# Order of the set-up before the first normalization of a two-layer conv/FFN kernel

## What is computed

```
x = x + L0_conv(_ln_c(x), w_d, w_u, w_r, w_l)
t = _to_tokens(x)
t = t + L0_ffn(_ln_t(t), gate_w, gate_b, weight1, weight2)
x = _from_tokens(t, x)
x = x + L1_conv(_ln_c(x), w_d, w_u, w_r, w_l)
t = _to_tokens(x)
t = t + L1_ffn(_ln_t(t), W, V, gamma, beta)
x = _from_tokens(t, x)
```

## Time and profile before

| | |
|---|---|
| median of 3 runs | 4314.11 us (4312.28 to 4323.86) |
| the profiled execution, span | 4315.0 us |
| PE busy / ACT busy / DVE busy | 97% / 47% / 31% of the span |
| chain that ended last | 93% on PE |
| first matmul on x | 20.16 us |
| first ACTIVATE of ACT | 22.49 us |
| first matmul of the sweeps | 144.54 us |

### The profile page before, as it was taken

One profiled execution on the slowest core, in us unless ns is written; L12 is line 12 of the kernel. 1 busy time (PEld: TensorE's weight loads), 2 busy tenths in 40 slices (PEclk: granted clock), 3 DMA queues, 4 the chain that ended last, 5 costly groups with the idle time before them and its releaser, 6 DMA issues.

```text
span 4315.0 us, 139757 instructions
## 1 busy us (share of the span) xinstructions
PE 4170.7 (97%) x57266; PEld 3076.9 (71%) x57266; DVE 1330.3 (31%) x2528; ACT 2016.0 (47%) x8972; POOL 119.6 (3%) x243
## 2 busy tenths in 40 slices
PE   7999999999989999999999899999999999999999
PEld 2799999995342699999995266666666666666665
DVE  3555533334555655533334700000000000000000
ACT  5002334334554102243344366666666666666666
POOL 1000000000000000000000000000000000000000
PEclk8899999999999999999999899999999999999999
DMA  5000000002447200000005400000000000000000
GB/s 138 17 0 0 0 0 0 0 0 74 133 113 216 61 0 0 0 0 0 0 0 143 124 15 21 15 21 21 15 21 21 15 21 21 15 21 21 15 21 18
DMA packets 178401, 144.32 MB, mean 33 GB/s; under 512 B 110910, under 2 KB 177502, under 8 KB 178014
## 3 DMA queue, kind: packets, MB, share of 16 engines
q1 hardware_dynamic: 178014, 138.21, 12.1%
HBM read 79.19 MB, written 58.98 MB: 32 GB/s over the span
## 4 chain that ended last, share of the span: by engine, by line
PE 93%; DVE 3%; issue 2%; ACT 2%; SPq 1%; DMA 0%; ACTq 0%; DVEq 0%; PEldq 0%
PE ps L930 22%; PE ps L767 21%; PE ps L745 18%; PE ps L835 16%; PE ps L830 3%; PE ps L571 3%; PE ps L563 1%; PE ps L582 1%; PE ps L592 1%; PE ps L718 1%; PE ps L606 1%; DVE rstd L1162 1%; PE ps L808 1%; PE ps L636 1%; PE ps L685 1%
## 5 line engine op out<-in xcount | busy, mean ns | idle before, releaser
L930 PEld LDWEIGHTS ps<-xl,vt 65*32 65x32 f32 x28800 | 1036.0, 108 | 717.0 <-ACT xl L1145 686.2
L1145 ACT ACTIVATE xl<-ps 64x8 f32<-64x8 f32 x7200 | 1176.5, 170 | 656.8 <-PE ps L930 652.8
L930 PE MATMUL ps<-xl,vt 65*32 65x8 f32 x28800 | 1422.6, 183 | 20.6
L835 PE MATMUL ps<-idle 128*32 128x256 bf16 (+1 forms) x5894 | 1374.9, 273 | 0.0
L767 PE MATMUL ps<-xl,taps 128*128 128x128 f32 (+2 forms) x7880 | 921.3, 280 | 4.7 <-DVE xl L1334 4.7
L767 PEld LDWEIGHTS ps<-xl,taps 128*128 128x128 f32 x7880 | 920.8, 191 | 5.6 <-issue 5.3
L745 PE MATMUL ps<-split 128*128 128x400 f32 x4140 | 781.0, 352 | 12.8 <-DVE split L1329 12.8
L745 PEld LDWEIGHTS ps<-split 128*128 128x128 f32 x4140 | 779.0, 190 | 16.5 <-issue 15.2
L1418 DVE TENSOR_TENSOR xl<-xl 64x320 f32<-64x320 f32 x180 | 125.1, 695 | 1709.1 <-PEq L934 1699.7
L1003 ACT ACTIVATE img<-xl 128x144 f32 x788 | 365.8, 464 | 556.5 <-DVE xl L1311 556.5
L835 PEld LDWEIGHTS ps<-idle 128*32 128x32 bf16 x5894 | 584.5, 99 | 22.1 <-issue 10.2
(11 more groups left out here) (153 smaller groups left out, 1685.0 us busy)
## 6 DMA issues: line engine op xcount, KB each, us to landing
ring<-in_x_dram SPq DMA_DIRECT2D x144, 200.0 KB, 3.7
x_dram<-sums SPq DMA_DIRECT2D x144, 200.0 KB, 3.2
t_dram<-sums SPq DMA_DIRECT2D x72, 200.0 KB, 3.6
ring<-t_dram SPq DMA_DIRECT2D x72, 200.0 KB, 3.9
ring<-x_dram SPq DMA_DIRECT2D x72, 200.0 KB, 3.7
xl<-x_dram SPq DMA_DIRECT2D x45, 320.0 KB, 4.6
out_dram<-xl SPq DMA_DIRECT2D x45, 320.0 KB, 3.5
img<-in_L_ffn_weight_dram SPq DMA_DIRECT2D x4, 512.0 KB
```

The costliest lines, as they stand in the source:

```text
L835: pe.matmul(PS[bank][0:32, 0:n], idle[:, 0:32], idle[:, 0:n], start=True, stop=True)
L930: last = pe.matmul(PS[2 * s + h][c * 32:(c + 1) * 32, t * HB:(t + 1) * HB], vt[:, c * 32:(c + 1) * 32], prev, start=False, stop=True, skip ...
L1145: act.activation(yb[0:64, s % 2, h * HB:(h + 1) * HB, t], PS[s % 2 * 2 + h][0:64, t * HB:(t + 1) * HB], ACT.Sigmoid).then_inc(step_y[h][s ...
```

## The change

- SP issues the x loads of the first norm first. The small loads that nothing needs early (gate_b, gamma, beta) come behind all x loads of that norm (`late_constants`, with a semaphore `late_dma`, for which ACT waits ahead of the second norm and DVE ahead of the batch norm).
- ACT issues gate_w, W and V and the four convolution weights from its own queue, then waits for `consts`, and runs one square root of one element (`warm`) ahead of the norm. It no longer waits for `taps_ready[0]` there.
- POOL fills `idle`, `ident`, `average` and `eps` and sets `consts`; then `pick` and `tables_ready`; then `gate`, `taps`, `fold`, `ones`, `pooled` and the diagonals of `fold`, and `tables_ready` again; then `spread32` as before.
- PE runs 12 idle matmuls behind `consts`, then waits for `centre_ready` and `tables_ready`, and enters the norm. The weight work is in `prepare_weights`, in five parts behind the units 2 to 6: the gate; W and V; nine taps; nine taps; the small product. The idle matmul behind the variances of the first norm runs only from unit 8 on.
- `row_squares` lies behind the weights in `xl`, and the tap transposes of layer 0 use banks 5, 6 and 7.

```diff
-        row_squares = [xl[:, j * CH:(j + 1) * CH] for j in range(SQUARES)]
+        row_squares = [xl[:, 4 * C * KT + j * CH:4 * C * KT + (j + 1) * CH] for j in range(SQUARES)]
...
+        def late_constants(sp):
             for q in range(4):
+                sp.dma_start(gbias[q * E:(q + 1) * E, :], gate_b.rearrange("(e a) -> e a", a=1)).then_inc(late_dma, 16)
+            for h in range(2):
+                sp.dma_start(half(gb, h)[:, 0:1], gamma.rearrange("(e a) -> e a", a=1)).then_inc(late_dma, 16)
+                sp.dma_start(half(gb, h)[:, 1:2], beta.rearrange("(e a) -> e a", a=1)).then_inc(late_dma, 16)
...
         @block.sync
         def _(sp):
-            sp.dma_start(graw[:, :], gate_w).then_inc(setup_dma, 16)
...
-            sp_norm(sp, 0)
+            sp_norm(sp, 0, meanwhile=lambda: late_constants(sp))
...
-            for buf, value in ((ident, 0.0), (average, 0.0), (fold, 0.0), (gate, 0.0), (taps, 0.0), (ones, 1.0),
-                               (pooled, 1.0), (idle, 0.0)):
-                alone(pool.memset(buf[:, :], value))
+            for buf in (idle, ident, average):
+                alone(pool.memset(buf[:, :], 0.0))
...
+            pool.affine_select(out=ident[:, :], in_=ident[:, :], compare_op=ALU.not_equal, fill=1.0, base=0,
+                               pattern=[[-1, 128]], channel_multiplier=1).then_inc(consts, 1)
+            alone(pool.memset(pick[:, :], 0.0))
+            for h in range(2):
+                alone(pool.memset(half(pick, h)[:, 126 + h:127 + h], 1.0 / C))
+            pool.sem_inc(tables_ready, 1)
+            for buf, value in ((gate, 0.0), (taps, 0.0), (fold, 0.0), (ones, 1.0), (pooled, 1.0)):
+                alone(pool.memset(buf[:, :], value))
...
-            if i == 0:
+            if i == 0 and n >= 8:
                 keep_clock(pe, 512, SPARE)
...
+        def prepare_weights(pe, part):
+            if part == 0:
+                pe.wait_ge(setup_dma, 16)
+                pe.transpose(PS[7][0:C, 0:E], graw[:, :], ident[0:E, 0:E]).then_inc(gate_t, 1)
+            elif part == 1:
+                pe.wait_ge(rdma, 32)
+                pe.wait_ge(gate_ready, 1)
+                for a in range(2):
+                    last = pe.transpose(PS[7][0:64, 64 + a * 64:128 + a * 64], wraw_r[:, a * 64:(a + 1) * 64], ident[0:64, 0:64])
+                last.then_inc(rnn_t, 1)
+            elif part < 4:
+                pe.wait_ge(rnn_w_ready, 1)
+                pe_taps(pe, 0, part - 2)
+            else:
+                pe.wait_ge(wcp[0], 6)
...
+                if i == 0 and 2 <= n <= 6:
+                    prepare_weights(pe, n - 2)
...
             pe.wait_ge(consts, 1)
-            pe.wait_ge(setup_dma, 80)
...
+            for _ in range(12):
+                keep_clock(pe, 512, SPARE)
             pe.wait_ge(centre_ready, 1)
...
+            pe.wait_ge(tables_ready, 1)
             pe_row_norm(pe, 0)
...
         @block.scalar
         def _(act):
-            act.wait_ge(setup_dma, 80)
+            act.dma_start(graw[:, :], gate_w).then_inc(setup_dma, 16)
+            act.dma_start(wraw_r[:, 0:64], rnn_w).then_inc(rdma, 16)
+            act.dma_start(wraw_r[:, 64:128], rnn_v).then_inc(rdma, 16)
+            load_taps(act, 0)
             act.wait_ge(consts, 1)
-            act.wait_ge(taps_ready[0], 1)
+            act.activation(warm[:, :], eps[0:1, 0:1], ACT.Sqrt)
             act_row_norm(act, 0)
...
+            act.wait_ge(late_dma, 128)
             act_token_norm(act, 1)
...
             dve.wait_ge(gate_t, 1)
+            dve.wait_ge(tables_ready, 2)
...
+            dve.wait_ge(late_dma, 128)
             link(dve.tensor_tensor(bnm[:, 6:7], bnm[:, 5:6], gb[:, 0:1], ALU.mult), 3)
```

More of the change, by code:

```diff
@@ L153, in b2_at @@
             return slots[0:1, 1, b, a:a + n * C]
+        late_dma = sem("late_dma")
         setup_dma, consts, gate_t, gate_ready = sem("setup_dma"), sem("consts"), sem("gate_t"), sem("gate_ready")
-        centre_ready, pick_ready, spread_ready = sem("centre_ready"), sem("pick_ready"), sem("spread_ready")
+        centre_ready, tables_ready, spread_ready = sem("centre_ready"), sem("tables_ready"), sem("spread_ready")
         wdma, wtr, wcp, taps_ready = ([sem(f"{n}{l}") for l in range(2)] for n in ("wdma", "wtr", "wcp", "taps_ready"))
@@ L199, in metaformer @@
         bn_std, rnn_c = sem("bn_std"), sem("rnn_c")
[L200 removed]
+        pool_done = sem("pool_done")
         passed = sem("passed")
@@ L498, in _ @@
                 alone(pool.memset(half(pick, h)[:, 126 + h:127 + h], 1.0 / C))
+            pool.sem_inc(tables_ready, 1)
+            for buf, value in ((gate, 0.0), (taps, 0.0), (fold, 0.0), (ones, 1.0), (pooled, 1.0)):
+                alone(pool.memset(buf[:, :], value))
+            for base in (0, 64, -64):
+                alone(pool.affine_select(out=fold[:, :], in_=fold[:, :], compare_op=ALU.not_equal, fill=0.5, base=base,
+                                         pattern=[[-1, 128]], channel_multiplier=1))
+            pool.sem_inc(tables_ready, 1)
             ones_at = sums[:, 0:5 * 128]
             alone(pool.memset(ones_at, 0.0))
-            pool.sem_inc(pick_ready, 1)
             for q in range(4):
@@ L514, in _ @@
             pool.wait_ge(ln[1].var, 2 * UNITS)
-            pool.memset(taps[:, :], 0.0).then_inc(taps_blank, 1)
-            pool.wait_ge(taps_blank, 1)
+            alone(pool.memset(taps[:, :], 0.0))
             place_taps(pool, 1)
@@ L535, in _, with tap_at, pe_taps @@
             stage_segment(pool, 0, 0, 0)
-        TAP_BANKS = (((4, 5, 6), (4, 5, 6)), ((2, 3, 4), (5, 6, 7)))
-        def pe_taps(pe, l):
+        TAP_BANKS = (((5, 6, 7), (5, 6, 7)), ((2, 3, 4), (5, 6, 7)))
+        NINTH = (256, 0)
+        def tap_at(l, a, k):
+            c = k % 4 * 128 + (NINTH[l] if k == KT - 1 else 0)
+            return PS[TAP_BANKS[l][a][k // 4]][0:64, c:c + 128]
+        def pe_taps(pe, l, a):
             pe.wait_ge(wdma[l], 64)
             wk = wraw[l].rearrange("p (a i k) -> p a k i", a=2, k=KT)
[L542 to L548, removed]
+            for k in range(KT):
+                if l == 0 and a == 1 and k % 4 == 0:
+                    pe.wait_ge(wcp[l], k // 4 + 1)
+                last = pe.transpose(tap_at(l, a, k), wk[:, a, k, :], ident[:, :])
+                if k % 4 == 3 or k == KT - 1:
+                    last.then_inc(wtr[l], 1)
         def variances(pe, i, n, squares):
@@ L672, in pe_token_norm @@
                     centre_and_project(n, 1)
+        def prepare_weights(pe, part):
[14 more added lines that the diff above has]
+                for h in range(2):
+                    last = pe.matmul(PS[7][h * 64:(h + 1) * 64, 192:256], half(centre, h)[:, h * 64:(h + 1) * 64],
+                                     half(wbd, h)[:, h * 64:(h + 1) * 64], start=True, stop=True)
+                last.then_inc(rnn_c, 1)
         def pe_row_norm(pe, i):
@@ L821, in pooling @@
             if g == NG - 1:
-                pe_taps(pe, 1)
+                for a in range(2):
+                    pe_taps(pe, 1, a)
             pe.wait_ge(pool_read, g + 1)
```

39 lines of the change are left out of this document (8 added, 31 removed).

## The result

The changed kernel takes 4289.22 us (median of 4 runs, 4286.89 to 4296.33), the kernel before 4316.10 us (median of 4, 4312.28 to 4323.86). The ratio is 0.9939, with a 95% interval of 0.9927 to 0.9951: 26.9 us, 0.62%, faster. The profiled execution of after took 4290.47 us, its span 4288.7 us. The two spans are 26.3 us apart.

The account below looks back on a forecast made before the run. Serial set-up, then x loads, then PE were taken as bounds; earlier means (13.8 us) and two table loads (1.3 us each), less 4.0 us in first units, gave 12.4 us gained: 4301.7 us, range 4294.5 to 4309.0 us.

Parts of the forecast that it names:

- What bounds the kernel now: First 145 us: serial set-up, x loads pace units 0 to 10, PE bounds from unit 12; root difference carries to the end.
- POOL, ACT and the weights' places: Set-up: `consts` at 3.57 us, ACT's issues end about 5 us, second table load goes; weights between units cost 3.5 us.
- The rival of dear issues: Norm start: x waits in shared engines or ACT's issues are dear; about 3 us less gained, 4304.7 us, chance 0.12.
- PE's entry: PE's start: 12 idle matmuls at 0.227 us take 2.7 us, so PE is free at 6.3 us.
- The rival of a start at 1.2 GHz: PE's start: idle matmuls take 5.4 instead of 2.7 us, first means at 9.0 us; 4303.8 us, chance 0.05.
- The transposes: Weight work between first-norm units: nine transposes cost PE 1.93 us, and late means delay later x loads.
- The trip of a load: First norm, units 0 to 10: means n + 3 start about 4.7 us after means n end.
- The clock: Behind the first root: PE's fall to 1.2 GHz is kept; a 10.2 us stretch costs some 3.5 us.
- Nothing changed behind it: Everything behind the sweeps' first matmul, itself forecast 12.4 us sooner near 132.1 us, stays unchanged.
- The slower rival: First units: clock falls and stays low until the idle matmuls ahead of the last group; 4351 us, chance 0.04.
- The rival of a drain: ACT's table switch costs a drain besides the load; 1.3 us more gained, 4300.4 us, chance 0.03.
- The rival of hidden transposes: First norm: transposes hide in PE's waits for loads; root at 27.2 us, 4298.2 us, chance 0.10.

Follow-up runs that it names:

- weights_behind_x: The changed kernel with the seven weight loads issued by SP behind the first six x loads, not by ACT: 4290.81 us, ratio 0.9932.
- no_idle: The changed kernel without the 12 idle matmuls at the start, 24 spare semaphore increments in their place: 4291.58 us, ratio 0.9934.
- before_again: The kernel before, unchanged, run once more: 4316.01 us, ratio 0.9995.
- no_warm_root: The changed kernel without the one-element square root ahead of the norm: 4293.80 us, ratio 0.9942.
- before_code_as_after: The kernel before with 8 idle matmuls instead of 16 and spare increments: one on PE, one on DVE, six on ACT; 4306.59 us, ratio 0.9983.
- weights_ahead: The changed kernel with all five parts of the weight work ahead of the first unit, behind the 12 idle matmuls: 4296.09 us, ratio 0.9957.

## Why the prediction was wrong, and where it was right

**What bounds the kernel now** stood. The set-up is serial, and the 13.4 us won at the first root were still there at the sweeps.

**POOL, ACT and the weights' places.** `consts` at 3.57 us as forecast. ACT's seven issues take 0.41 to 0.67 us each and end at 5.08 us (about 5 forecast), one table load at 5.11 us, none behind it. The rival of dear issues falls. The small late loads and `place_taps` (ends at 25.3 us, 27 forecast) lie outside the path to the reciprocal at 30.40 us.

**PE's entry was wrong.** Forecast 2.7 us for 12 idle matmuls and the first means at 6.35 us; measured 4.34 us and 7.84 us. PE starts at 1.2 GHz. In weights_behind_x the twelve take 5.30 us, 0.44 us each, and in no_idle the first means run at half rate. Here my reading of the trace failed: I took a granted clock of 1.00 at 12 us and a mean of 0.227 us as the engine's state at its first matmul. The column shows 1.00 up to the first recorded change, also where the durations show the lower level. In before the first record is a rise at 16.24 us, behind 4 us of transposes at the low rate and just ahead of the idle matmuls at 16.60 us, which so took 3.63 us. In before_again the rise is recorded at 20.16 us, and they took 5.30 us. In after it is recorded at 6.79 us, in the middle of the twelve. The Trainium skill, "TensorE: Matmul & The Clock Gate", section "What's actually happening", has the throttled state as the default. These durations agree with it, and the prediction's sentence that the trace speaks against it was wrong. The rival of a start at 1.2 GHz, given 0.05, is what happened at this point: it had the first means at 9.0 us, which weights_behind_x nearly reaches with 8.81 us.

**The transposes were wrong the other way.** Nine were to take 1.93 us each time; they take 1.20 us, because the earlier trace rows gave the low rate and after runs them at the high one. Unit 2 was to have its means at 9.9 us and had them at 11.67 us, 2.20 us of it waiting for its load, beyond even the late bound of 11 us. The errors cancel:

| means of unit | forecast | measured |
|---|---|---|
| 0 | 6.35 | 7.84 |
| 2 | 9.9 | 11.67 |
| 5 | 17.3 | 17.75 |
| 7 | 22.4 | 21.43 |
| 10 | 28.05 | 27.23 |
| first root | 30.7 | 29.75 |

The late start and the late x together make unit 2 1.8 us late; each nine transposes give 0.7 us back. The trip of a load held: unit 10 starts 4.9 us behind the end of the means of unit 7 (22.36 us), where 4.7 us were forecast. From the first means to the root the sum had 24.35 us, and it took 21.91 us. The root is 13.4 us sooner (12.4 forecast). That this term is so near was luck: it is made from two errors that cancel. Against the mean of the old starts the step, read at the reciprocal, is 15.4 us. The starting point of the sum, the root at 43.14 us, was taken from one execution, the quickest of six.

**The clock.** A fall was kept behind the root: it came, at 34.1 us, for 6.8 us, and was 10.2 us long before. The low stretches that began before the sweeps sum to 37.6 us instead of 47.8 us. From the root to the sweeps another 3.2 us were gained. The difference in the clock is large enough for them, but no run separates the two. That the difference at the root is carried unchanged to the end was wrong there. By the same sum all six profiles with the old start have 44 to 51 us of low clock, the eight with the changed start 27 to 44 us. Which part of the change moves the falls is not settled: no edit here moved them alone, and two kernels whose root came 1.9 and 8.1 us later than after's had the least of it.

**"Nothing changed behind it" is the step that failed by the most.** Two column sweeps are 3.5 and 3.6 us shorter, because the code in front of them has another length. The prediction put this at nothing, and no rival held it. The account is: 13.4 to 15.4 us at the root and some 7 us from code places. The 4 to 6 us that are left of the 26.9 us I put down to the clock's low stretches and to the chance of single executions; this rest was not measured by itself.

The slower rival, PE kept at 1.2 GHz by the norm's own work, is excluded: in no_idle that work raised the clock on its own. The rival of a drain finds no support in the two loads of no_warm_root. The rival of hidden transposes, with a root at 27.2 us, was not tested by itself, and the root came at 29.75 us.

## What to carry to other kernels

An edit ahead of all loops can change the time of every loop behind it: compare the length of each stage in both traces, count the matmuls in equal stretches of it, and pad the old kernel to the new code lengths before the gain is put down to the edit. Take the clock from the durations of a known operation, not from the granted clock alone at the start of a kernel, and take a start time from more than one profiled execution. Here 13.4 us won in a serial set-up came through to the PE-bound stage behind it, but a microsecond or two at one point of it could not be found again in the whole time.

## What the runs showed of the chip that was not expected

- Where a loop's code lies can cost time on PE and DVE: a shift of 15 instructions on PE makes 3.6 us on a column sweep of 224.0 us (855 or 868 matmuls in 100 us), and one instruction on DVE makes 3.7 us on another (3.0 us in before_code_as_after). Six on ACT make none there. By the lengths of single steps it comes once for each turn of the moved loop: 0.04 us a turn on PE, 0.08 us on DVE.
- The profile shows PE at 100% busy and a granted clock of 1.00 in the slow and in the fast sweep.
- The granted clock reads 1.00 ahead of its first recorded change while PE runs at 1.2 GHz: 0.44 us for a matmul of 512 columns there, 0.22 us for a transpose that takes 0.13 us later.
- The clock falls for 3.4 to 13.7 us at places of the norms that shift with small edits, and the sum of the stretches that began before the sweeps ran from 27.3 to 51.2 us over kernels that compute the same. In weights_ahead a root that is 8.1 us later was followed by sweeps that begin 0.4 us sooner.
